# Last stage of an adaLN block with routed experts: the residual tiles read earlier, and part of the pair sums moved to TensorE

## The reference

```python
gate_scores = jax.nn.sigmoid(gate_logits + balance_bias)
topk_scores, topk_idx = jax.lax.top_k(gate_scores, TOP_K)            # TOP_K = 2
topk_scores = topk_scores / (topk_scores.sum(-1, keepdims=True) + 1e-06)
...
h = jax.nn.silu(jnp.einsum('td,edh->teh', xf, W1))
out = jnp.einsum('teh,te,ehd->td', h, combine, W2)
...
x = x + gb * _L0_ffn_ref(h, L0_ffn_Wg, L0_ffn_balance_bias, L0_ffn_W1, L0_ffn_W2)
```

## Time and profile before

| | us |
|---|---|
| three timed runs | 1644.54, 1652.25, 1651.16 |
| their median | 1651.16 |
| the profiled execution | 1648.23 |
| its span, from the first to the last instruction | 1645.6 |
| of this the last stage, from its first DMA issue at 1567.59 | 78.0 |

### The profile page before, as it was taken

The page is one execution under the profiler, slowest core; times in us unless marked ns, Lnnn a source line. Parts: engine busy times, 40 slices in busy tenths (PEclk is TensorE's granted clock), DMA queues, the critical chain, the costliest instruction groups (busy, mean ns, idle before and its releaser), DMA issues. The chain is left out here.

```text
span 1645.6 us, 27981 instructions
## 1 busy us (share of the span) xinstructions
PE 1410.0 (86%) x8713; PEld 1006.4 (61%) x8713; DVE 1252.1 (76%) x2928; ACT 792.3 (48%) x1414; POOL 733.0 (45%) x683
## 2 busy tenths in 40 slices
PE   4679998899999889999988999999973999999900
PEld 3557665566566566656655666665441999999800
DVE  3578787787778778777867877789757777777778
ACT  4324546634354663334456434445513666666622
POOL 3244355342435434243543333364425677777500
PEclk8899999999999999999999999999995999999955
DMA  6555564445355444535534453553744455445389
GB/s 220 170 162 155 153 164 112 117 123 155 104 152 159 119 117 123 156 104 143 155 104 130 131 156 91 130 138 83 279 150 167 160 185 185 142 147 172 117 327 371
DMA packets 141491, 256.14 MB, mean 156 GB/s; under 512 B 17200, under 2 KB 81200, under 8 KB 141376
## 3 DMA queue, kind: packets, MB, share of 16 engines
q1 hardware_dynamic: 113280, 178.70, 36.9%
q0 software_dynamic: 13792, 47.72, 8.6%
q10 hardware_dynamic: 14304, 28.32, 5.1%
HBM read 167.34 MB, written 85.75 MB: 154 GB/s over the span
## 5 line engine op out<-in xcount | busy, mean ns | idle before, releaser
L682 ACT ACTIVATE probs<-ring 128x1024 f32<-128x1024 f32 (+3 forms) x384 | 310.8, 812 | 188.5 <-PE ring L536 116.0
L501 PE MATMUL ring<-stack_t 96*128 96x512 f32 (+3 forms) x768 | 295.6, 409 | 18.8 <-DMA stack_t<-stack_dram 15.6
L479 PE MATMUL ring<-w_parts,h_hi 128*128 128x384 f32 x1024 | 277.0, 352 | 9.8 <-DVE neg_max L863 4.0
L866 DVE CUSTOM_DVE_ANT_0 ring<-ring,later_b 128x384 f32<-128x384 f32 (+3 forms) x512 | 247.9, 497 | 26.1 <-PE ring L501 25.1
L501 PEld LDWEIGHTS ring<-stack_t 96*128 96x128 f32 x768 | 141.1, 192 | 169.9 <-issue 61.5
L1150 POOL TENSOR_TENSOR prob_sum<-prob_sum,probs 128x1024 f32<-128x1024 f32 (+3 forms) x128 | 230.0, 1797 | 29.1 <-ACT probs L682 28.5
L1163 POOL TENSOR_TENSOR rope_a<-rope_a,rope_b 128x256 f32<-128x256 f32 x128 | 93.4, 730 | 334.6 <-DVE rope_b L936 334.5
L530 PE MATMUL ring<-stack_t 128*128 128x512 f32 (+3 forms) x768 | 210.6, 356 | 26.1 <-ACT probs L682 17.2
L479 PEld LDWEIGHTS ring<-w_parts,h_hi 128*128 128x128 f32 x1024 | 190.9, 198 | 20.0 <-issue 13.2
L863 DVE TENSOR_REDUCE neg_max<-ring 128x1 f32<-128x512 f32 x256 | 175.0, 684 | 17.1 <-PE ring L501 14.8
L479 PE MATMUL ring<-w_parts,h_lo 128*128 128x384 f32 x512 | 177.4, 346 | 0.0
(11 more groups left out here) (192 smaller groups left out, 2385.6 us busy)
## 6 DMA issues: line engine op xcount, KB each, us to landing
stack_t<-stack_dram SPq DMA_DIRECT2D x384, 128.0 KB, 3.3
stack_dram<-parts SPq DMA_DIRECT2D x64, 512.0 KB, 2.9
w_parts<-w_dram SPq DMA_DIRECT2D x96, 192.0 KB, 3.5
w_sb<-y_dram SPq DMA_DIRECT2D x32, 512.0 KB, 6.6
w_sb<-w SPq DMA_DIRECT2D x22, 512.0 KB, 5.7
x_in<-x SPq DMA_DIRECT2D x32, 256.0 KB, 3.7
x<-x SPq DMA_DIRECT2D x32, 256.0 KB, 3.7
x_dram<-x SPq DMA_DIRECT2D x32, 256.0 KB, 2.9
```

The source lines that it names most:

```text
L479: mm = nc.tensor.matmul(ring[:, BANK[use], 0:384], lhs[:, c, cols], rhs[:, c, :], start=(k == 0), stop=(k == len(products) - 1))
L501: nc.tensor.matmul(ring[:, BANK[use], 0:width], stack_t[0:MROW, i % 2, 0, h, qt * P:qt * P + P], stack_t[0:MROW, i % 2, 1, h, kc * 512:kc ...
L682: nc.scalar.activation(probs[:, step % PROBS, :, q0:QC], ring[:, bank:bank + 2, q0:QC], ACT.Exp)\
L866: nc.vector.tensor_tensor_reduce(ring[:, BANK[use], 0:width], ring[:, BANK[use], 0:width], later_b[:, QC - width:QC], -1.0, 3e38, ALU.add, ...
```

## The change

It has two parts. First, SP reads all remaining residual tiles (20 to 31) in the expert stage as well: FREED becomes 20, and the places of experts 2, 3 and 4 are used when DVE has passed slot 66, 67 and 68. The last stage then has no residual reads.

Second, for ten tiles (2, 5, 8, ..., 29; `BY_PE`) the sum of the two weighted row sets is no longer made by DVE's L1653. ACT now multiplies both row sets by their weights (two operations instead of one), and PE adds them with two matmuls against the identity matrix into a PSUM bank (`sum_ps`, two banks in turn). DVE's multiplication by gb reads that bank. ACT's output DMA now belongs to the tile three before (LAG = 3) and not two.

```diff
@@ the reads ahead of time @@
-            EARLY, FREED = 12, 8
+            EARLY, FREED = 12, TT - 12
             most = -(-B * L // P)
+            past = [most * (e + 1) if e < 2 else 2 * most + e for e in range(FREED // 4)]
...
-            x_early += [tiles[:, 2 * e + n, :] for e in range(2) for tiles in (w1_tiles, w2_tiles) for n in range(2)]
+            x_early += [tiles[:, 2 * e + n, :] for e in range(FREED // 4) for tiles in (w1_tiles, w2_tiles) for n in range(2)]
...
-                            sp.wait_ge(w2_lo_r, most * ((t - EARLY) // 4 + 1))
+                            sp.wait_ge(w2_lo_r, past[(t - EARLY) // 4])
                             sp.dma_start(x_early[t], x1_dram[t, :, :]).then_inc(early_in, 16)
...
@@ the last stage @@
+            BY_PE = [t for t in range(2, TT - 2) if t % 3 == 2]
+            nth = {t: n for n, t in enumerate(BY_PE)}
...
+            sum_ps = part.enter_context(nc.psum_tensor("sum_ps", [P, 2, D], f32))
...
-                        if t >= EARLY:
-                            sp.dma_start(x_late[:, t - EARLY, :], x1_dram[t, :, :]).then_inc(late_in[k], 16)
+
+                @block.tensor
+                def _(pe):
+                    for n, t in enumerate(BY_PE):
+                        pe.wait_ge(m_a, n + 1)
+                        pe.wait_ge(m_b, t + 1)
+                        if n >= 2:
+                            pe.wait_ge(m_g, BY_PE[n - 2] + 1)
+                        for half in range(2):
+                            mm = nc.tensor.matmul(sum_ps[:, n % 2, :], ident_f[:, :], y_pair[:, t % DEPTH, half, :],
+                                                  start=(half == 0), stop=(half == 1))
+                        mm.then_inc(m_s, 1)
 
                 @block.scalar
                 def _(act):
-                    for t in range(TT + 2):
+                    LAG = 3
+                    for t in range(TT + LAG):
                         if t < TT:
                             k = t % DEPTH
                             act.wait_ge(y_in[k], 16 * (t // DEPTH + 1))
+                            if t in nth:
+                                nc.scalar.activation(y_pair[:, k, 0, :], y_pair[:, k, 0, :], ACT.Copy, scale=weight[:, t, 0:1])\
+                                    .then_inc(m_a, 1)
                             nc.scalar.activation(y_pair[:, k, 1, :], y_pair[:, k, 1, :], ACT.Copy, scale=weight[:, t, 1:2])\
                                 .then_inc(m_b, 1)
-                        if t >= 2:
-                            u = t - 2
+                        if t >= LAG:
+                            u = t - LAG
                             act.wait_ge(m_x, u + 1)
                             act.dma_start(out_tiles[u, :, :], y_pair[:, u % DEPTH, 0, :]).then_inc(out_s[u % DEPTH], 16)
...
-                        dve.wait_ge(m_b, t + 1)
-                        nc.vector.scalar_tensor_tensor(out=y, in0=y, scalar=weight[:, t, 0:1], in1=y_pair[:, k, 1, :],
-                                                       op0=ALU.mult, op1=ALU.add).then_inc(m_w, 1)
-                        dve.wait_ge(m_w, t + 1)
-                        nc.vector.tensor_tensor(y, y, gb_b[:, t // NT, :], ALU.mult).then_inc(m_g, 1)
+                        if t in nth:
+                            dve.wait_ge(m_s, nth[t] + 1)
+                            summed_y = sum_ps[:, nth[t] % 2, :]
+                        else:
+                            dve.wait_ge(m_b, t + 1)
+                            nc.vector.scalar_tensor_tensor(out=y, in0=y, scalar=weight[:, t, 0:1], in1=y_pair[:, k, 1, :],
+                                                           op0=ALU.mult, op1=ALU.add).then_inc(m_w, 1)
+                            dve.wait_ge(m_w, t + 1 - sum(n <= t for n in BY_PE))
+                            summed_y = y
+                        nc.vector.tensor_tensor(y, summed_y, gb_b[:, t // NT, :], ALU.mult).then_inc(m_g, 1)
                         dve.wait_ge(m_g, t + 1)
-                        if t >= EARLY:
-                            dve.wait_ge(late_in[k], 16 * ((t - EARLY) // DEPTH + 1))
-                        x_at = x_early[t] if t < EARLY else x_late[:, t - EARLY, :]
-                        nc.vector.tensor_tensor(y, y, x_at, ALU.add).then_inc(m_x, 1)
+                        nc.vector.tensor_tensor(y, y, x_early[t], ALU.add).then_inc(m_x, 1)
```

More of the change, by code:

```diff
@@ L1610, in adaln_block @@
             DEPTH = 8
-            EARLY += FREED
+            BY_PE = [t for t in range(2, TT - 2) if t % 3 == 2]
+            nth = {t: n for n, t in enumerate(BY_PE)}
             y_pair = w1_sb[:, E // 2:E, :, :].rearrange("p e c f -> p (e c f)").rearrange("p (t k d) -> p t k d", t=DEPTH, d=D)
-            x_late = w2_tiles[:, E:E + TT - EARLY, :]
             y_in = [sem(f"y_in{k}") for k in range(DEPTH)]
-            late_in = [sem(f"late_in{k}") for k in range(DEPTH)]
             out_s = [sem(f"out_s{k}") for k in range(DEPTH)]
-            m_b, m_w, m_g, m_x = sem("m_b"), sem("m_w"), sem("m_g"), sem("m_x")
+            m_b, m_w, m_g, m_x, m_a, m_s = sem("m_b"), sem("m_w"), sem("m_g"), sem("m_x"), sem("m_a"), sem("m_s")
+            sum_ps = part.enter_context(nc.psum_tensor("sum_ps", [P, 2, D], f32))
             out_tiles = out.rearrange("b (t p) d -> (b t) p d", p=P)
```

## The result

The changed kernel is slower: 1656.63 us, median of 20 runs (1650.1 to 1659.92), against 1652.03 us of the kernel before, also of 20 runs. The ratio is 1.0028, with a 95% interval of 1.0018 to 1.0038, or +4.6 us. The prediction had 1645.7, in a range from 1639.5 to 1651.

A forecast was written before the change was run, and what follows sets the result against it. DVE was taken as the bound for 24 tiles of the last stage, the DMA engines for the rest. -3.5 - 6.9 + 3.1 + 0.6 + 1.0 = -5.7 us, taken as -5.5, gave 1645.7 us, range 1639.5 to 1651.

The forecast's parts named there:

- The reads: Twelve residual reads moved from last stage to expert stage: DVE gets back 3.5 us of late waiting, at no cost there.
- DVE's saving: Last stage: each weighted sum moved to PE saves DVE 0.69 us, ten save 6.9; multiplying from PSUM costs no more.
- Tile 2: First tile summed by PE in the last stage: DVE waits 3.1 us for it, whatever the clock does later.
- Tile 8: Last stage, first pair behind a wait of SP: PE's sum ready at 1591.1, DVE there at 1590.5, 0.6 us of waiting.
- The circle between ACT, PE and DVE: Last stage: PE's sum comes 5.4 us after DVE ends tile t-4, covered by 5.65 us of DVE work.
- so I allow 1.0 us more over tiles 11 to 29: Last stage: allowance for DVE waiting because later pairs are issued behind outputs leaving up to 2.4 us later.
- rival 1: Last-stage ring turns too slowly: 18.8 us for a PE tile if landings exceed about 10.5 us; 7.1 slower, 1658; chance 0.08.
- the medians are mostly queueing: Argument against slow ring turns in the last stage: shortest landings are 3.6 and 2.0 us, and 3.15 MB less is queued.
- The data bound: Last-stage transfers: 25.17 MB at 344 GB/s take 73.2 us, 5.7 less than 78.9, given as agreeing with the sum.
- the better variant: PE's clock rises in the last stage: sums take 1.95 us, waits after the first PE tile are covered, total -7.3 us.

The follow-up runs named there:

- after_depth12: The changed kernel with 12 pairs of buffers in the ring instead of 8, LAG 3 and PE's sums kept: ratio 0.9955 to the kernel before.

## Why the prediction was wrong

- **The reads** were right: 3.5 us forecast for DVE's late waits, 3.2 us measured alone. In the expert stage PE stayed busy, 15.00 of 15 us around the moved reads.
- **DVE's saving** was right: 0.69 us a tile, and reading PSUM costs nothing (689 ns against 691 from SBUF).
- **Tile 2** was right: 3.1 us forecast, 3.5 measured. **Tile 8** came out at 0.67 for 0.6, with some luck: counted from the start of the stage its pair came 0.6 us later than forecast, and so did DVE.
- **The circle between ACT, PE and DVE** was right: a cover of 5.65 us against 5.4, and with 12 pairs DVE waited at no tile behind tile 2. With 12 pairs and LAG 2, where the cover is 4.2, it paid 1.2 us a tile.
- **The failed step** is "so I allow 1.0 us more over tiles 11 to 29". It measured 15.0 - 3.5 - 0.7 = 10.8 us, because the pairs came too late. I had looked at LAG only as cover for PE. I overlooked that the output of tile u stands behind the multiplication of tile u+3 in ACT's stream, and so behind the landing of that pair. The chain of before had shown this at 1624.38, with an output issued on the landing of a pair, in the stretch that I put down to the residual reads alone. A turn of the ring is then two landings for 8 - LAG tiles, and the change took one of six away. With 12.3 us of landings that was 2.05 us a tile before, just under DVE's 2.11, and 2.3 or more after, just when DVE's own pace fell to 1.9 and every third tile came to need its pair 4.3 us earlier. That PE's time is in the ring's long way as well is rival 1, next.
- **Rival 1** is half right. It named the ring, and its turn of 18.8 us, with a PE tile's own work in it, is in the chain once, with 19.05 us; from there to the last of PE's tiles the chain takes the short way, which it didn't have. Its condition, two landings above 10.5 us, was met with 6.3 + 5.2 = 11.5. That condition was even too mild, since it set the turn against DVE's old pace: at the new one, 8 x 1.88 = 15.1 us, the turn of an ordinary tile (15.1) fills the time already. Its 1658 came near the measured 1656.6, though DVE's part was 75.5 us with the wait of tile 2 in it and not 78.3. No run tells what each of the two ways cost by itself.
- **The landings.** I gave rival 1 0.08 because "the medians are mostly queueing" and 3.15 MB less would be queued. They fell only from 12.3 to 11.5 us together. The Trainium skill has a fit for one DMA issued from GpSimd in "DMA: Bandwidth & Descriptors", section on the anatomy of one DMA on the SWDGE path, 2.0 us and bytes over 436e3; by it an estimate for DMAs of these sizes is 3.2 us for a pair and 2.6 for an output. These come from SP and ACT, and the shortest landings are 3.7 and 2.0, so the trace agrees only roughly; the shortest output lies below the estimate. So the medians are well above what a transfer takes by itself, and yet the circle pays them in full. That this is so because each landing shares the DMA engines with the other outputs and pairs in flight is my reading; no run tests it alone.
- **The data bound** I gave as agreement, 5.7 us, was none: it subtracted a time at 344 GB/s from one at 359, and took for granted that the changed stage would ask for data as fast. With the circle of five tiles the stage moved its 25.2 MB at 305 GB/s on average, with 12 pairs at 354.
- **The clock** rose as I had it in the better variant, but for one sum: 0.64 was granted in the window from 1577 to 1587, and the sum at 1584.98, right behind that of tile 2, took 1.95 us. After 5.82 us of idleness the next took 3.75, and 0.50 was granted from 1597 and from 1617. The Trainium skill says in "TensorE: Matmul & The Clock Gate", Part 1, that activity releases the throttle and idleness brings it back; the trace agrees for these sums. The late pairs aren't the reason that the variant failed. With 12 pairs, where DVE waited for none of them, the eight sums from tile 8 on took 2.39 to 3.75 us, five of them 3.4 or more, though from tile 11 on PE stood idle for only 1.8 to 2.9 us before each. With 10 pairs one sum of eight took 1.96. So the clock didn't stay up at that pace either.

## What to carry to other kernels

When a DMA is issued from an engine that also computes, list everything that stands ahead of it in that engine's stream and what each waits for: the issue inherits those waits, and the ring of buffers loses as many places as the issue is late. Moving work to an idle engine in a pipeline costs lead, not only time: ask how much earlier its operands must be there, and whether the ring can deliver that. And before a lag is tuned for one purpose, write down the other circle that it is part of; here LAG 2 starves PE and LAG 3 the ring, and two to four more buffers paid for LAG 3. Issuing the outputs from an engine that doesn't compute would test the order in ACT's stream more directly; no run here does it.

## What the runs showed of the hardware

- The DMA share doesn't tell whether the DMA engines could move more. Windows of the changed kernel show shares of 0.94, 0.98 and 1.01 at 347, 350 and 339 GB/s, where the kernel before had 1.05 at 414. With 12 pairs (after_depth12; 40 equal slices of its last stage, share in tenths and GB/s) the same traffic went at more than 400 GB/s through most of the stage, without any residual reads:

```profile
DMA  3999999999999999999999999999999997425212
GB/s 94 394 369 413 410 385 322 394 415 419 418 413 410 417 422 410 421 407 423 409 419 411 409 408 417 408 419 414 416 417 414 419 403 275 164 84 211 113 74 108
```

- In the kernels with PE's sums, a deeper ring got more data per us and longer landings at once. The medians for a pair and an output were 6.3 and 5.2 us in the changed kernel at a mean of 305 GB/s, 6.8 and 6.4 with 12 pairs at 354, and 8.1 and 7.6 with 12 pairs from tile 5 on at 361.
- Two accumulating matmuls of 512 columns against the identity took 3.75 us in float32 at the lower clock, 1.95 us where it had risen, and 1.19 us in float32r, at the lower clock.
